# Causal mask of the transposed scores: two added matmuls per head group, or a select by GpSimd on the probabilities

## The reference, cut to what matters

```python
s = jnp.einsum('bhqd,bhkd->bhqk', q, k) / math.sqrt(DH)
alibi = slopes[:, None, None] * (i - j)
mask = jnp.triu(jnp.full((T, T), -jnp.inf, dtype=jnp.float32), 1)
s = s + alibi[None] + mask
p = jax.nn.softmax(s, axis=-1)
o = jnp.einsum('bhqk,bhkd->bhqd', p, v).transpose(0, 2, 1, 3).reshape(B, T, E)
```

## Time and profile before

| | us |
|---|---|
| median of three timed runs (2305.91 to 2318.0) | 2306.05 |
| the profiled execution's own time | 2315.66 |
| its span in the profile | 2313.9 |

### The profile page before, as it was taken

One profiled execution on the slowest core, in us unless ns is written; L12 is line 12 of the kernel. 1 busy time (PEld: TensorE's weight loads), 2 busy tenths in 40 slices (PEclk: granted clock), 3 DMA queues, 4 the chain that ended last, 5 costly groups with the idle time before them and its releaser, 6 DMA issues. The chain is left out here.

```text
span 2313.9 us, 52728 instructions
## 1 busy us (share of the span) xinstructions
PE 1965.5 (85%) x18758; PEld 1405.2 (61%) x18759; DVE 1723.1 (74%) x3717; ACT 1398.9 (60%) x2736; POOL 1036.8 (45%) x1231
## 2 busy tenths in 40 slices
PE   2889989899862999378799999999999999549999
PEld 1666666666561666145577777676767777426665
DVE  4778888788791444468678787879696977679997
ACT  1666666666562444267668696868787878344443
POOL 4435534355014000488747576657575663132222
PEclk9999999999955999689999999999999999869999
DMA  7000000000033332002100000000000000100000
GB/s 241 2 1 2 2 2 2 2 2 2 3 128 127 98 91 79 12 11 35 22 1 2 2 2 2 2 1 2 1 2 2 2 2 2 38 1 14 18 18 23
DMA packets 53114, 57.77 MB, mean 25 GB/s; under 512 B 7121, under 2 KB 47217, under 8 KB 52897
## 3 DMA queue, kind: packets, MB, share of 16 engines
q1 hardware_dynamic: 46240, 45.00, 6.2%
q0 software_dynamic: 6656, 9.85, 2.0%
HBM read 36.22 MB, written 18.61 MB: 24 GB/s over the span
## 5 line engine op out<-in xcount | busy, mean ns | idle before, releaser
L371 PE MATMUL a_bank<-w_in_sb,xnT_sb 128*128 128x512 f16 x1152 | 293.7, 394 | 33.7 <-DVE t_buf_sb L579 26.4
L1116 DVE TENSOR_REDUCE neg_max_sb<-a_bank 128x1 f32<-128x128 f32 (+3 forms) x512 | 236.1, 485 | 92.6 <-PE a_bank L896 88.7
L531 DVE TENSOR_REDUCE neg_max_sb<-a_bank 128x1 f32<-128x128 f32 (+3 forms) x512 | 236.1, 482 | 92.6 <-PE a_bank L288 91.1
L1039 ACT ACTIVATE probT_sb<-a_bank 128x512 f32<-128x512 f32 (+1 forms) x384 | 198.8, 526 | 145.3 <-PE a_bank L919 140.5
L442 ACT ACTIVATE p_hi_sb<-a_bank 128x384 f16<-128x384 f32 (+1 forms) x384 | 205.3, 535 | 120.7 <-PE a_bank L297 119.0
L434 ACT ACTIVATE prob_sb<-a_bank,neg_max_sb 128x128 f32<-128x128 f32 (+3 forms) x512 | 261.4, 543 | 23.9 <-DVE neg_max_sb L531 23.0
L538 DVE TENSOR_TENSOR p_lo_sb<-a_bank,p_hi_sb 128x384 f16<-128x384 f32 (+1 forms) x384 | 228.0, 595 | 59.7 <-ACT p_hi_sb L442 56.1
L453 ACT ACTIVATE stack_sb<-a_bank 128x1024 f16<-128x1024 f16 (+1 forms) x256 | 211.4, 826 | 7.0 <-PE a_bank L342 6.6
L297 PE MATMUL a_bank<-ident_f_sb,prob_sb 128*128 128x128 f32 x1280 | 206.4, 276 | 3.7 <-DVE p_lo_sb L538 3.1
L707 POOL TENSOR_TENSOR rope_w_sb<-t_buf_sb,sin_sb 128x256 f32<-128x256 f32 x128 | 146.0, 1140 | 134.7 <-DVE t_buf_sb L579 132.2
L371 PEld LDWEIGHTS a_bank<-w_in_sb,xnT_sb 128*128 128x128 f16 x1152 | 104.9, 100 | 143.0 <-DVE t_buf_sb L579 34.2
(11 more groups left out here) (268 smaller groups left out, 5613.3 us busy)
## 6 DMA issues: line engine op xcount, KB each, us to landing
sorted_rows<-zeros_sb SPq DMA_DIRECT2D x1, 4992.0 KB, 21.6
x_in_sb<-sorted_rows SPq DMA_DIRECT2D x39, 128.0 KB, 2.1
sorted_results<-y_moe_sb SPq DMA_DIRECT2D x39, 128.0 KB, 1.7
x_sb_sb<-L_attn_x SPq DMA_DIRECT2D x8, 512.0 KB, 10.7
w_raw_sb<-L_ffn_gate_bank SPq DMA_DIRECT2D x8, 512.0 KB, 3.6
w_raw_sb<-L_ffn_up_bank SPq DMA_DIRECT2D x8, 512.0 KB, 4.7
w_raw_sb<-L_ffn_down_bank SPq DMA_DIRECT2D x8, 512.0 KB, 5.8
out<-x_sb_sb SPq DMA_DIRECT2D x32, 128.0 KB, 1.7
```

Of the source, the lines that this page charges most:

```text
L371: last = pe.matmul(out, xnT[:, x, c, j * P:(j + 1) * P], w["in"][:, w_, c, cols], start=k == 0, stop=k == len(terms) - 1)
L531: last = dve.tensor_reduce(neg_max[:, i:i + 1], S[(3 * h + g) % 2][:, off:off + L], AX.X, ALU.max, negate=True)
L1039: act.activation(probT[:, (h // 4) % 2, h % 4, T_AT[r]:T_AT[r + 1]], ST[(3 * h + r) % 2][:, 0:T_AT[r + 1] - T_AT[r]], ACT.Exp).then_inc(s_ ...
L1116: last = dve.tensor_reduce(neg_max[:, h % 2, i:i + 1], S[(3 * h + g) % 2][:, off:off + L], AX.X, ALU.max, negate=True)
```

## The change

The second scores are no longer masked: the matmul at L919 goes, and L917 closes its bank alone. POOL gets a new function, `mask_probs`, ahead of its `take` in each slot: it waits until ACT has written the exponentials of the group, sets those of later keys to zero in place with `affine_select` on each diagonal block (128 keys by 128 queries, f32), and raises a new semaphore, `s_keep`. `pv` waits for `s_keep` where it waited for ACT's `s_exp`.

```diff
-                pe.matmul(out, stack[0:K0, h % 4, T + kt * P:T + (kt + 1) * P], stack[0:K0, h % 4, kt * P:T],
-                          start=True, stop=False)
-                last = pe.matmul(out[:, 0:P], mask[:, :], ident_b[:, :], start=False, stop=True)
+                last = pe.matmul(out, stack[0:K0, h % 4, T + kt * P:T + (kt + 1) * P], stack[0:K0, h % 4, kt * P:T],
+                                 start=True, stop=True)
...
-            wait(pe, s_exp, 12 * Q + 10 + part)
+            wait(pe, s_keep, 12 * Q + 10 + part)
...
+        def mask_probs(b, h, r):
+
+            wait(pool, s_exp, b * GROUPS + 3 * h + r + 1)
+            p = probT[:, (h // 4) % 2, h % 4, :]
+            for kt in KT_GROUPS[r]:
+                block_ = p[:, KT_AT[kt]:KT_AT[kt] + P]
+                last = pool.affine_select(block_, block_, [[1, P]], ALU.is_ge, 0.0, base=0, channel_multiplier=-1)
+            last.then_inc(s_keep, 1)
...
         def slot(cur, off, k, last):
             b = cur + off
+            if 0 <= k - LAG_S < GROUPS:
+                mask_probs(b, (k - LAG_S) // 3, (k - LAG_S) % 3)
             for kind, ahead, *a in work(k - LAG_WV, last):
```

More of the change, by code:

```diff
@@ L810, in attention0 @@
     s_exp = sem("probsT_ready")
+    s_keep = sem("probsT_masked")
     s_pv = sem("quad_pv_ready")
```

## The result

The changed kernel takes 2350.25 us (median of four runs, 2347.14 to 2354.76). Before, beside it, took 2309.24 (four runs). The ratio is 1.0173 with a 95% interval of 1.0137 to 1.0209, so the change costs 40 us, between 32 and 48. The profiled execution took 2348.78 us, 33 us above the one of before.

A forecast was written before the change was run, and what follows sets the result against it. PE, busy for 90%, was taken to set the pace in the first attention. Two places costing 43 and 32 us, less 13 us for saved mask rows, made +62 us on 2306, so 2368 us; range 2322 to 2470.

The forecast's parts named there:

- the pieces' stretches: Slots 31 to 40, seven batches, and 1 to 10, eight batches: selects queue between POOL's takes, costing 43 + 32 us.
- just in time: POOL's fourth take, behind three more selects, was to end at 340.85, when slot 45's stack fill needs it at 340.9.
- t: Price of one 128x128 f32 select on POOL: taken as 0.40 us, with 0.30 and 0.67 kept as bounds.
- the first place: `pv` of slot 41 waits for POOL; slot 45 reached 4.35 us later, 6.2 with the clock, x 7 = 43 us.
- the second: Up to `pv` in slot 17, POOL owes four takes and 18 selects: 4.0 us x 8 = 32 us.
- the 1.83 us charged: Once per batch, for a lower TensorE clock after the stall at slot 41: 4.60 us less 2.77 for two slots.
- the prediction's 5.2: PE's time in us from slot 41's `pv` to slot 45's fill, less the wait and the saved mask rows.
- the term of 13 us for 20 slots: PE's gain from dropped mask rows in slots 17 to 32 and 45 to 50: 20 x 0.08 x 8 = 13 us.
- The casts: DVE's small casts slow while POOL works: 0 to 77 us of DVE time, taken as 0 because DVE idles 19%.
- (a): Rival: a select of 1.14 us makes POOL the bound, +272 us, 2578; chance 0.18 with what leads to it.
- (b): Rival: the stalls replace PE's other waits, 6.4 us per batch, so not slower: 2317 or 2299 us; chance 0.08.
- (c): Rival: the stall stays small, first place 1.6 us, second 0.64 + 2t = 1.4, sum +9, 2315 us; chance 0.06.

The follow-up runs named there:

- e2: The changed kernel with each select replaced by a memset of one column of a spare tile, same queue and waits; 2323.12 us, 1.0064.
- e3: The changed kernel with every select done twice, the first time into a spare tile; 2406.78 us, 1.0421.
- e4: The kernel before, mask rows kept, with POOL also running the selects between spare tiles and nobody waiting for them; 2335.9 us, 1.0112.
- e1: The changed kernel without the selects, so no mask at all, `pv` waiting for ACT's exponentials as before; 2294.96 us, 0.9941.
- e10: The kernel before with pieces three slots earlier, `pv` parts three slots later and the projection of slot 76 at 88; 2302.09 us, 0.9951.
- e8: The kernel before, mask rows kept, with pieces three slots earlier and `pv` parts three slots later; 2308.39 us, 0.9994.

## Why the prediction was right, and where its sizes were off

**The mechanism held.** Two places, the pieces' stretches, lose; the rest does not. `pv` waits for POOL in slots 41, 5 and 17 and at no other part. The order of POOL's queue gives the time: 335.78 + 3 x 4.0 + 9 x 0.245 = 349.99, and `pv` starts at 350.04. The fourth take, worked out as "just in time", ends at 353.50 + 1.14 = 354.64, and the fill at 356.59 waits for nothing. e2, e3 and e4 tie this to the queue. The load itself is free where no take stands in the queue: slots 17 to 29, with 16 selects and no take, need 19.36 us after and 19.35 in e1, without any select.

**The step that was mis-sized: t.** I took 0.40 us, with 0.30 as the lower bound; it is 0.245. The bound was the duration of a row on 128 columns, where the queue pays the step between starts. By the low end of what the Trainium skill (GPSIMD Engine Reference, section "Performance pitfalls for Q7 kernels") states, 1.03 cycles per element, the estimate was 0.30 us for the duration, and the trace agrees: 0.291. With t = 0.245 the prediction's own formulas give 2.95 + 1.83 = 4.8 at the first place, 344.26 + 16.0 + 18 x 0.245 - 363.46 = 1.2 at the second, and 7 x 4.8 + 8 x 1.2 - 13 = +30 us. The trace has +31. By place: slot 29 to 45 took 356.59 - 328.66 = 27.93 us against 23.36, so 4.6; slot 45 to 17 took 27.81 against 26.91, so 0.9. The waits of slot 17, expected at 2 us, are 0.18 for the same reason.

**The clock.** The low clock behind slot 41 came, in all seven batches, and cost less than the 1.83 us charged: slots 41 to 45 took 356.59 - 350.04 = 6.55 us, 1.3 above the prediction's 5.2. Some 0.2 of the 1.83 was no clock: slot 29 in the earlier trace rows holds a part 0 of `pv`, which takes PE 0.99 us to the next row, and slot 44 a part 1, which takes 0.79. The wall itself was 0.3 larger than the formula's, 21.38 - 17.29 = 4.1 us against 3.8, so that the 4.6 above agrees with 4.8 in part by luck.

The low clock of before, in slots 25 to 29 of six batches, is gone in five of them in the profile after, which the prediction did not count. What it is worth is read from e4, which keeps the mask rows and has none there; from slot 17 to 29 it takes 19.79 us against 21.40, so 1.6 us per batch:

```profile
302.61 1.06 PE L934 MATMUL a_bank<-probT_sb,v_stage_sb 128*32 128x512 f32 x8
...
322.40 1.07 PE L934 MATMUL a_bank<-probT_sb,v_stage_sb 128*32 128x512 f32 x8
```

In the profiles the two low clocks cancel, nearly.

**The mask rows.** At 0.06 us a row I put them at no more than 31 us. They give 13 us on the median (e1), and in slots 17 to 29 0.43 us (19.79 in e4, 19.36 after): 0.036 us per slot, where I had 0.08. Over all 48 slots 0.036 makes 1.7 us per batch, or 14 in eight, which fits the 13. PE loses part of the rest to other waits; in e1, which runs ahead, the fill waits 9.5 us in seven for POOL, where it waited 4.5 before. So the term of 13 us for 20 slots was nearer to 6; the vanished low clock filled its place in the profile. That +30 and +31 agree so closely is luck to that extent.

**The casts.** No cost was taken, and none is seen: DVE's busy time is 1718.5 us against 1723.1, and L1125 still has its median at 178 ns over 100 to 560 us, though single ones last longer:

```profile
L1125 DVE CAST max_parts_sb<-neg_max_sb x99: 176/178/602, 99.8 to 559.9; 128x4 bf16<-128x4 f32 x99
```

DVE does end more of PE's waits than before, which the prediction named as a sign against it: those over 100 to 560 us sum to 43 us, and to 37 before. But they sum to 43 in e1 too, which has no select, so they come with the missing mask rows and not with the casts.

**The rivals.** (a) falls with t = 0.245 (0.291 as a duration), far below the 0.61 at which POOL bounds every slot and the 1.14 and 1.47 that it was given; (b) falls with the other waits of PE, which grew a little; (c) falls with a wait of 3.90 us and a low clock behind it. The 0.64 of (c) was not worked out: the earlier trace rows give 344.26 + 4.0 - 346.98 = 1.28, by which (c) comes to 2321 us in place of 2315, and falls all the same.

**What stays open.** The medians differ by 41 us, the profiled executions by 33. Both profiles of before (2315.66 and 2319.65 us) lie above the medians of the timed runs, and both have the low clock in six batches, some 10 us. If most timed runs of before lack it, the difference between the kernels is 31 + 10 = 41, which fits; and the mean granted clock of its runs goes with their times, 0.942 in the two fastest of 23 (2302.3 and 2302.7) and 0.934 and 0.933 in the two slowest (2318.17 and 2318.34). But timed runs leave only that mean: where their clock was low is argued here, not shown.

## What to carry to other kernels

Work given to an engine with idle time is free only if nothing with a deadline stands behind it in the queue: write out that engine's queue from one deadline to the next and add up, since the busy share (39% here) says nothing of it. For such sums take the step between starts of neighbouring instructions, not the duration of one. Where the order is the trouble, moving the deadline by a few slots may be worth more than the instruction that is replaced; e10, which keeps the mask rows and only moves work between slots, is faster than both kernels.

## What the runs showed of the hardware

A select by GpSimd over 128x128 f32 steps at 0.245 us, and as a duration it is no slower than a one-input TENSOR_SCALAR on 128 columns (291 ns against 296). Slots 25 to 29 had a stretch of low clock in six batches of both profiles of before. Ahead of the one in the earlier trace rows PE was busy for 2.64 of 4 us and waited for DVE three times, for 0.96 us at the longest. The changed kernel stayed at 1.00 in the same slots in five of these six batches, with PE busy for 2.47 and 2.98 of 4 us; e1, e8 and e10 have no low clock between 100 and 600 us. So such a stretch can vanish with a change elsewhere, and it has to be counted on both sides of a comparison; what decides it is not shown here.
